# A transformer block on one core: weights awaited one by one, two input buffers, and new written-out orders of work

## The reference

```python
x = x + 0.5 * ffn(layernorm(x))        # "p"
x = x + attention(layernorm(x))        # "a"
x = x + 0.5 * ffn(layernorm(x))        # "q", the same weights as p
```

## Time and profile before

| what | us |
|---|---|
| median of 3 runs | 1632.12 (1631.79 to 1634.74) |
| the profiled execution's own time | 1630.6 |
| its span, first to last instruction | 1628.5 |
| PE busy | 1504.9 (92%) |
| DVE busy | 1203.6 (74%) |
| ACT busy | 1118.3 (69%) |
| POOL busy | 816.9 (50%) |

### The profile page before, as it was taken

The page is one execution under the profiler, slowest core; times in us unless marked ns, Lnnn a source line. Parts: engine busy times, 40 slices in busy tenths (PEclk is TensorE's granted clock), DMA queues, the critical chain, the costliest instruction groups (busy, mean ns, idle before and its releaser), DMA issues.

```text
span 1628.5 us, 40855 instructions
## 1 busy us (share of the span) xinstructions
PE 1504.9 (92%) x13632; PEld 1330.6 (82%) x13632; DVE 1203.6 (74%) x4771; ACT 1118.3 (69%) x3400; POOL 816.9 (50%) x789
## 2 busy tenths in 40 slices
PE   0867999999999999999999999999999999999876
PEld 0656788889888888988888898888888888889665
DVE  4455787887878788687878878787887878786644
ACT  2346777777767767786766777776777777677643
POOL 1325464555556465465546555554555555464433
PEclk9989999999999999999999999999999999999888
DMA  3135453635454353535436363544526353454401
GB/s 99 53 109 145 121 153 96 165 118 150 122 141 141 99 155 115 160 121 150 131 99 161 101 167 127 145 124 115 158 88 181 118 145 117 132 144 120 138 17 65
DMA packets 270052, 203.86 MB, mean 125 GB/s; under 512 B 154474, under 2 KB 224516, under 8 KB 269844
## 3 DMA queue, kind: packets, MB, share of 16 engines
q1 hardware_dynamic: 266352, 201.14, 43.5%
q10 hardware_dynamic: 3460, 0.04, 0.1%
q0 software_dynamic: 32, 0.07, 0.0%
HBM read 146.06 MB, written 42.47 MB: 116 GB/s over the span
## 4 chain that ended last, share of the span: by engine, by line
PE 57%; DVE 22%; issue 8%; ACT 5%; POOL 5%; DMA 2%; SPq 2%; DVEq 0%; ACTq 0%; POOLq 0%
PE gb L759 9%; PE gb L761 8%; PE gb L760 8%; PE yb L759 6%; PE yb L761 6%; PE yb L760 6%; PE ptb L818 4%; PE sb_ L809 3%; PE cxb L836 3%; DVE pr L642 3%; DVE xn L589 2%; POOL pr L379 2%; ACT xn L472 2%; POOL sq L390 2%; DVE xl L667 1%
## 5 line engine op out<-in xcount | busy, mean ns | idle before, releaser
L396 POOL TENSOR_TENSOR gl<-ag,gh 128x512 fp32r<-128x512 f32 x288 | 382.5, 1333 | 218.8 <-ACT gh L498 218.6
L379 POOL TENSOR_TENSOR pr<-pr,rinv 128x512 f32<-128x512 f32 x256 | 300.8, 1175 | 345.0 <-DVE rinv L650 341.5
L453 ACT ACTIVATE pr<-pr,mx 128x128 f32<-128x128 f32 x1024 | 397.0, 395 | 41.5 <-DVE mx L642 41.5
L759 PE MATMUL yb<-w2h,gh 128*128 128x256 f32 x1152 | 335.2, 291 | 5.5 <-POOL gl L396 5.4
L760 PE MATMUL yb<-w2h,gl 128*128 128x256 f32 x1152 | 321.8, 279 | 0.0
L761 PE MATMUL yb<-w2l,gh 128*128 128x256 f32 x1152 | 321.5, 279 | 0.0
L642 DVE CUSTOM_DVE_ANT_0 pr<-sb_,mask 128x128 f32<-128x128 f32 x1024 | 235.8, 285 | 97.8 <-issue 94.8
L498 ACT ACTIVATE gh<-ag 128x512 fp32r<-128x512 f32 x288 | 179.4, 627 | 126.8 <-DVE ag L711 86.4
L759 PE MATMUL gb<-xh,w1h 128*128 128x512 f32 x576 | 247.8, 430 | 9.2 <-DVE qkl L622 7.9
L504 ACT ACTIVATE tt<-gb,b1half 128x512 f32<-128x512 f32 x288 | 195.9, 680 | 83.0 <-PE gb L761 81.2
L711 DVE SCALAR_TENSOR_TENSOR ag<-tt,ag 128x512 f32<-128x512 f32 x288 | 233.5, 815 | 2.6
(11 more groups left out here) (138 smaller groups left out, 2782.9 us busy)
## 6 DMA issues: line engine op xcount, KB each, us to landing
gate<-gates_pair SPq DMA_DIRECT2D x256, 256.0 KB, 3.7
ks<-qk_dram SPq DMA_DIRECT2D x256, 128.0 KB, 2.9
qs<-qk_dram SPq DMA_DIRECT2D x512, 64.0 KB, 2.5
qk_dram<-qkh SPq DMA_DIRECT2D x64, 256.0 KB, 4.0
qk_dram<-qkl SPq DMA_DIRECT2D x64, 256.0 KB, 4.1
vb<-va SPq DMA_DIRECT2D x32, 384.0 KB, 6.9
xres<-L_attn_x_dram SPq DMA_DIRECT2D x16, 512.0 KB, 3.8
out_dram<-xres SPq DMA_DIRECT2D x16, 512.0 KB, 3.4
```

The costliest lines, as they stand in the source:

```text
L379: nc.gpsimd.tensor_tensor(pr[:, k], pr[:, k], rinv[:, k, :].unsqueeze(2).to_broadcast([P, NP, P]), ALU.mult).then_inc(a_pn, 1)
L396: nc.gpsimd.tensor_tensor(gl[:, k, :], ag[:, k, :], gh[:, k, :].bitcast(F32), ALU.subtract).then_inc(f_gl, 1)
L453: nc.scalar.activation(pr[:, k, r, :], pr[:, k, r, :], ACT.Exp, bias=mx[:, k, r:r + 1], scale=-1.0, accum_out=rsum[:, k, r:r + 1]).then_in ...
L759: nc.tensor.matmul(dst, ah, bh, start=start, stop=False, **kw)
```

## The change

- `ORDER` has new texts for the repeating part, and a `HEAD` and a `TAIL`, in which each step is written with its own image (`pH3=1` is expert 3 of image 1). `run` emits HEAD, then the repeating part without the steps that HEAD and TAIL name, then TAIL. The longest lead of p over q is two images as before.
- U steps come in pairs: only U1, U3, ... U15 are listed, and each does its own and the one before (`UG = 2`). A pair waits for the later copy phj. The number of matmuls is unchanged. In the repeating order PE has U1, U3, U5, U7, U9, U11 each alone among other steps and U13 and U15 side by side; before it had U5 and U6, and U14 and U15 side by side and twelve others alone.
- NPR = 3 and NPT = 4; two input buffers (NXI = 2) with a semaphore each, so that x[1] is loaded at the start; attention's rows have a buffer axn of their own.
- Each group of weights has its own semaphore and is split by a step in the orders. Small loads are reordered on ACT's queue: the router's weights first, then expert bias and b1. The output bias goes over SP, last, and `raw` lies in va.
- In the head, pY0 of image 0 comes right behind its pC, ahead of pH1; X, L and H0 of image 1 come between the Y4 to Y8 of image 0. In the tail's last ffn, qY0 comes ahead of qC, and DVE does qa0 and qg0 ahead of qR2.

```diff
-        NG, NTT, NPR, NPT, NBANK = 2, 2, 2, 2, 3
-        YB2 = 4
+        NG, NTT, NPR, NPT, NBANK, NXI, NX1, LEAD = 2, 2, 3, 4, 3, 2, 2, 2
+        YB2, UG = 4, 2
...
+            head, tail = (fixed(text[engine]) for text in (HEAD, TAIL))
+            apart_ = set(head + tail)
+            for s, b in head:
+                step(s, b)
+            for i in range(-B, 2 * B):
+                for s, off in words(ORDER[engine]):
+                    if 0 <= i + off < B and (s, i + off) not in apart_:
                         step(s, i + off)
+            for s, b in tail:
+                step(s, b)
...
-            act.wait_ge(w_raw, 16 * (E + 7))
-            for dst, src in splits(w1h, w2h, wah):
-                nc.scalar.activation(dst, src, ACT.Copy).then_inc(w_hi, 1)
+                if s[:2] == "Wh":
+                    k = s[2:]
...
+                        act.wait_ge(w_in[WK.index(k)], 16 if k in ("1s", "2s", "2r") else 32)
+                        nc.scalar.activation(dst, src, ACT.Copy).then_inc(w_hi, 1)
...
-                    act.wait_ge(f_g1, 16 * max(2 * b, 1))
+                    wait(act, a_xt, 2 * b)
...
-            pe.wait_ge(w_lo, NSPLIT + 2)
-            pe.wait_ge(w_prep, 6)
-            pe.wait_ge(w_zero, 5)
+            def weights(k, first):
+                if first:
+                    pe.wait_ge(w_lo, lo_done(k))
...
                     pe.wait_ge(a_ph, NJ * b + j + 1)
...
+                    for w in range(j % NW - UG + 1, j % NW + 1):
+                        k = (NJ * b + c * NW + w) % NPT
...
+                        mm.then_inc(a_pv, 1)
```

More of the change, by code:

```diff
@@ L14 @@
 NEG = -1e30
[L19 to L24, removed]
@@ L51 @@
-"""
+ORDER = {
+    "PE": """
+P10-6 aX0-5 U9-6 aX1-5 S12-6 qY2-7 P11-6 S13-6 qY3-7 Q00-5 Q01-5 S14-6 pL-4 qY4-7 qH5-7 qH6-7 Q10-5 P12-6
+S15-6 U11-6 V0-5 P13-6 qH7-7 qH8-7 qY5-7 P14-6 qY6-7 P15-6 pH0-4 Q11-5 qY7-7 S0-5 qY8-7 pC-4 S1-5 U13-6
+U15-6 V1-5 S2-5 pY0-4 P0-5 O0-6 S3-5 pH1-4 P1-5 O1-6 S4-5 pH2-4 U1-5 pH3-4 S5-5 pH4-4 pY1-4 P2-5 pH5-4 pY2-4
+qX0-6 P3-5 qX1-6 S6-5 pY3-4 U3-5 pH6-4 pY4-4 qL-6 pY5-4 pH7-4 P4-5 S7-5 pH8-4 P5-5 qH0-6 pY6-4 U5-5 S8-5
+P6-5 qC-6 S9-5 pY7-4 P7-5 S10-5 pY8-4 qH1-6 S11-5 qH2-6 U7-5 qY0-6 pX0-3 pX1-3 P8-5 qH3-6 P9-5 qY1-6 qH4-6
@@ new lines @@
+S9=0 P7=0 S10=0 U7=0 P8=0 S11=0 S12=0 P9=0 aX0=1 aX1=1 pC=2 P10=0 U9=0 pY0=2 S13=0 P11=0 Q00=1 Q01=1 S14=0
+P12=0 pH1=2 S15=0 P13=0 U11=0 V0=1 Q10=1 P14=0 Q11=1 P15=0 U13=0 pH2=2 U15=0 pY1=2 V1=1 O0=0 O1=0 pY2=2
+pH3=2 pH4=2 S0=1 pH5=2 S1=1 qX0=0 qX1=0 S2=1 P0=1 S3=1 pY3=2 qL=0 P1=1 S4=1 pH6=2 U1=1 P2=1 S5=1 pY4=2 P3=1
+pY5=2 U3=1 pH7=2 P4=1 S6=1 pH8=2 qH0=0 P5=1 S7=1 pY6=2 U5=1 qC=0 S8=1 P6=1 pY7=2 S9=1 P7=1 S10=1 U7=1 pY8=2
+S11=1 qH1=0 qH2=0 qY0=0 pX0=3 pX1=3 P8=1 qH3=0 P9=1 qH4=0 qY1=0
+""",
+    "ACT": """
@@ L215, in wait, with run @@
                 eng.wait_ge(s, value)
-        def run(order, step):
-            for i in range(-3, B + 3):
-                for s, off in words(order):
-                    if 0 <= i + off < B:
+        def run(engine, step):
+            head, tail = (fixed(text[engine]) for text in (HEAD, TAIL))
[5 more added lines that the diff above has]
+                    if 0 <= i + off < B and (s, i + off) not in apart_:
                         step(s, i + off)
+            for s, b in tail:
+                step(s, b)
         def value_of(w):
@@ L245, in note @@
                 users.append((s, b))
-        run(ORDER_PE, note)
+        run("PE", note)
         def bank(s, b):
@@ L325, in step @@
                         .then_inc(a_vs, 16)
-            run(ORDER_SP, step)
+            run("SP", step)
             sp.wait_ge(x_out, 16 * B)
@@ L505, in step @@
                                          bias=b1half[:, e:e + 1], scale=0.5).then_inc(f_t, 1)
-            run(ORDER_ACT, step)
+            run("ACT", step)
         @block.vector
@@ L724, in step @@
                             ALU.mult, ALU.add).then_inc(f_res, 1)
-            run(ORDER_DVE, step)
+            run("DVE", step)
         @block.tensor
@@ L772, in step @@
                     c, u = int(s[1]), int(s[2])
+                    weights("qk", b == 0 and s == "Q00")
                     pe.wait_ge(a_xl, 2 * b + 2)
```

413 lines of the change are left out of this document (287 added, 126 removed).

## The result

The kernel after takes 1585.6 us in the median of 4 runs (1583.0 to 1587.6), the kernel before 1632.0 beside it: ratio 0.971, 95% interval 0.969 to 0.973, so 46 us faster. 1570 was predicted with a range from 1548 to 1604: inside, but 15.6 us too low.

A forecast was written before the change was run, and what follows sets the result against it. The rounds were taken as bound by PE. Span 1628.5 - 23 (start) - 34 (rounds) - 4.5 (tail) = 1567, 2.1 around it, 1569; the runs' median lies 1.5 higher: 1570 us, range 1548 to 1604 for 8 in 10.

The forecast's parts named there:

- The round: The repeating round between V1's of successive images: 91.0 us instead of 93.44, 34 us gained over 14 rounds.
- 7 x 0.14 + 4 x 0.19 = 1.8: PE time saved a round: seven fewer U groups at 0.14 us, four fewer U's right behind transposes at 0.19.
- Idle time: PE's idle time in a round: 1.1 us instead of 1.74, bounds 0 to 3.5.
- rival B: In the rounds, the new orders' stalls give back what pairs save; round stays 93.4, time 1604 us; chance 0.2.
- The head: Start of the kernel to V1 of image 1: V1 at 169, 23 us gained, bounds 13 and 30.
- lies beside w1 low: At the start, the root on POOL (1.64 us) runs beside DVE's split of w1 low, adding nothing to the sum.
- The tail: From V1 of image 15 to the end: 4.5 us gained, bounds 0 and 8.
- qY0 ahead of qC: In the last ffn: costs the gates up to 3 us, takes the same work out behind them, nothing net.
- pairs take 1.4 there: In the tail, pairs of U's were to take 1.4 us more off.
- C: Rival: PE hardly waits, round 90.0, and the start gains its full 30 us; time 1550 us; chance 0.15.
- D: Rival: at the start DVE's queue makes C wait for b2 and 1r anyway, head gains nothing; 1593 us; chance 0.1.
- E: Rival: slower, DVE operations with two SBUF inputs fall on POOL's in the rounds; 1680 us; chance 0.05.

The follow-up runs named there:

- Run 1: The kernel after with each pair of U's taken apart, the first U two entries earlier (U14 and U15 stay side by side): 1619.2 us.
- Run 3: The kernel before with NPR 3 and NPT 4, and each even U moved next to the odd one behind it: 1622.0 us.
- Run 7: The kernel after with DVE's wait for b1 and expert bias, and the halving of b1, moved into the bias-table step: 1580.5 us.
- 11: The kernel after with qC ahead of qY0 for the last image and DVE's wait for the first biases moved later: 1582.3 us.
- 12: The kernel after with the kernel before's relative order from iteration 20 on (U in pairs) and DVE's wait for the first biases later: 1571.4 us.
- 4: The kernel after with the TAIL texts empty, so that ORDER runs to the end: 1588.1 us.
- 5: The kernel after with qC of the last image ahead of qY0 in PE's tail: 1581.5 us.
- 6: The kernel after with qC ahead of qY0 for the last image, and that image's x2 in a free input buffer: 1586.0 us.
- 8: The kernel after with aX0 and aX1 of image 0 ahead of pC and pY0 of image 1 in PE's head: 1588.2 us.
- 9: The kernel after with all remaining steps from iteration 20 on in the kernel before's relative order, U still in pairs: 1576.8 us.
- 10: The kernel after with the kernel before's relative order starting a little before V1=15, one iteration later than in run 9: 1580.4 us.

## Why the prediction was right, and where it was off

**The round was right.** Predicted 91.0 us with PE busy 89.9 and 1.1 idle; measured 91.04, 89.94 and 1.10. Run 1 shows that the pairs make most of it. The size of their part was put together wrongly: I had 7 x 0.14 + 4 x 0.19 = 1.8, and the split kernel gives 2.13 to 2.19. The price is one of each group, about 0.3, with a third of it on the step behind, which I could not see in a price per step; the second term, on P's that no longer stand ahead of a U, was part of the same thing and not another one. The old busy time a round was also 92.28, not 91.70, since my mean held the last round. The two errors nearly cancel (-2.3 busy instead of -1.8).

**Idle time:** the three waits of the earlier trace rows were to shrink to 1.1 us a round together, and did, two of them to nothing. That they would not grow was the part that I chose without a row. Run 3 shows how much hung on it: with the old order, pairs leave 2.64 us idle and the mean round at 93.4, the round of rival B, 0.5 us of it by spells at the lower clock. B had 0.2 and would have been right for the old order.

**The head** was costed at -23 and brought -21.6. The marks up to S0 are 4 to 8 us late (first matmul 21.3 for 16.5, C 39.8 for 35.8, S0 109.4 for 101.6), and S0 to V1=1 took 61.4 for 67, so errors of 8 and 6 us cancel, and that the sum came out within 1.5 us is luck. The first is the one named in the text as a condition: DVE's first step waits for b1, and b1 came at 15.1, not at 10.5, a microsecond beyond even the upper of the bounds 6 and 14. Run 7 takes that wait away and the first matmul comes at 16.9. Of C's lateness, a further 0.9 us is the wait of DVE for the root on POOL, at 3.74 for 1.64; "lies beside w1 low" was taken as free. The Trainium skill (SBUF — State Buffer, "Who interferes with whom"), cited in the prediction for the rounds, names this pairing; the row agrees. The runs also say which of the two has to begin first: in runs 7, 11 and 12 w1 low began 0.25 to 0.26 us behind the root, and they took 1.64 and 2.29 us, as long as apart; where it began 0.04 ahead, as in the kernel after and in the seven other runs with this start (1, 4, 5, 6, 8, 9 and 10), the root took 3.74. Between C and S0 I allowed 13 us of waits; 69.6 us of span less 52.8 of work make 16.8, the second wait for a C alone being 6.1.

**The tail is the step that failed.** "I take 4.5 for the tail, bounds 0 and 8": V1=15 to the end was to fall from 128.0 to 123.5 and rose to 132.8. The reading that failed is "qY0 ahead of qC costs the gates up to 3 and takes the same work out from behind them: nothing net". Run 5 shows that it costs 3.0 net. The 5.9 us that the stretch behind O0=15 lost can be followed along its chain: the first transposes come 11.5 us behind O0 instead of 9.6, because DVE waits for the store of image 14's x2, which is issued 2.2 us later against O0 (1.4 shown in run 6); C comes 18.7 behind them instead of 14.9, 2.4 of that by Y0, 1.1 by the cast beside gl0 and some 0.4 by ACT's order, and for these last two the sum had no term; and the rest takes 34.6 instead of 34.4. Up to O0=15, where I forecast 65, it was 68.0, 1.1 less than before instead of some 4.5. That pairs take 1.4 there fell: run 9 has pairs and the old order, and the same 69.1 and 59.0 as before. PE waits for chains of small steps there, so its work is no term of the sum. The other term, 4 us more work ahead of qC, was not tried by itself; with the same TAIL this stretch took 65.1 in run 7, at a clock of 0.90 instead of 0.87.

**The last full round** was no step of mine. I divided 1308 us by 14 and took all rounds as equal. It was 85.75 and became 93.04; with the new ORDER it would have been 87.0 (run 4), so the TAIL text costs 6.0 there. In the sum, 1.5 us of the 16 missing belong to the head, 3.5 to the 13 rounds (3.0 of them to the first, at a clock of 0.95), and 11.3 to the stretch from V1=14 on (225.9 for 91.0 + 123.5). Run 9, with the same steps left at V1=14, shows that 215.1 was to be had.

**The rivals.** B and C fell with the round of 91.04. D, that the head gains nothing, fell with V1=1 at 170.8. E fell with line 887's 826 ns. What came was none of them but the forecast with a tail that lost instead of winning.

## What to carry to other kernels

Cutting the work of the bounding engine pays only as far as the engines beside it are ahead at the places where it now comes earlier: pairs alone gave 0.3 us of the 1.6 that they freed in a round (0.9 where the clock stayed up), and the full 2.1 with an order made for them. Before a mean over rounds is used, look at the first and the last by themselves, and cost the end of a pipeline as chains of waits, not as work. A step moved ahead of the one that the longest chain goes through is not neutral, even when the same work lies between.

## What the runs showed of the hardware

- A group of matmuls with 32-column weights among 128-column ones costs about 0.3 us beyond itself, about a third each before, in and behind the group; in the rounds 2.13 us for seven groups.
- A hole of 2 to 3 us in PE was followed by a stretch at 1.2 GHz whose length varied between kernels with the same instructions there: a granted clock of 0.93 or of 0.50 in the 10 us behind it, 4.2 us of difference in one round.
- The same two holes of PE of 0.8 us each, at the same place in every round of run 3, were followed by a spell at 1.2 GHz in three rounds of ten: 94.2 to 94.9 us instead of 92.75.
- A root on POOL over 128x8 took 3.74 us beside a subtraction of 128x2048 on DVE, and 1.64 in the kernel before. It took 1.64 too where the subtraction began 0.25 to 0.26 us behind it and not 0.04 ahead (runs 7, 11 and 12).
- A cast of 128x32 on DVE that began 0.05 us behind a subtraction of 128x512 on POOL took 1.25 us, and 0.18 without it (run 9).
